# A recurrent mixing block on one core: first sequence in halves, its difference on VectorE, loads in one queue, a new order on all engines

## The reference

```
xn = layernorm(x)                          # over the 128 channels
shifted = xn moved down by one position
k, v, r = mix(xn, shifted, coefficient) @ Wk, Wv, Wr      # r goes through a sigmoid
wkv = recurrence over the 512 positions in k and v (running maximum, numerator, denominator)
s = (r * wkv) @ Wo
h = relu(xn @ w1[0] + b1[0])               # 128 -> 512; the routing weights are 1 for expert 0, 0 for the others
g = silu(layernorm(xn + h @ w2[0] + b2[0]) * gamma + beta)
out = x + s * g
```

## Time and profile before

| What | us |
|---|---|
| median of 3 runs (112.02 to 112.39) | 112.1 |
| span of the profiled execution, first to last instruction | 110.7 |
| PE busy / PE weight loads busy | 101.9 / 56.7 |
| DVE busy | 96.0 |
| ACT busy | 94.3 |
| POOL busy | 66.0 |

### The profile page before, as it was taken

One profiled execution on the slowest core, in us unless ns is written; L12 is line 12 of the kernel. 1 busy time (PEld: TensorE's weight loads), 2 busy tenths in 40 slices (PEclk: granted clock), 3 DMA queues, 4 the chain that ended last, 5 costly groups with the idle time before them and its releaser, 6 DMA issues. The chain is left out here.

```text
span 110.7 us, 1604 instructions
## 1 busy us (share of the span) xinstructions
PE 101.9 (92%) x336; PEld 56.7 (51%) x336; DVE 96.0 (87%) x199; ACT 94.3 (85%) x155; POOL 66.0 (60%) x104
## 2 busy tenths in 40 slices
PE   4997799997999999999999999999999999999660
PEld 4993335553465445553675553674554566435230
DVE  1647989979999999799988989999999897899980
ACT  1425087899999998999899999999999999999940
POOL 3009998986746469459999998743819403360000
PEclk9999999999999999999999999999999999999998
DMA  3999200000000000000002110000000002203134
GB/s 98 284 314 288 61 3 0 0 6 0 0 3 3 0 0 0 0 0 0 0 0 95 46 57 0 0 0 0 3 0 0 3 0 95 81 14 95 46 101 143
DMA packets 9450, 5.09 MB, mean 46 GB/s; under 512 B 481, under 2 KB 9185, under 8 KB 9441
## 3 DMA queue, kind: packets, MB, share of 16 engines
q1 hardware_dynamic: 8880, 4.59, 14.7%
q10 hardware_dynamic: 560, 0.40, 1.3%
HBM read 2.89 MB, written 2.10 MB: 45 GB/s over the span
## 5 line engine op out<-in xcount | busy, mean ns | idle before, releaser
L638 PE MATMUL bank<-hid,w_c 128*128 128x512 f32 x64 | 31.1, 592 | 0.0
L589 PE MATMUL bank<-mixed,w_in 128*128 128x512 f32 x48 | 24.1, 599 | 0.8 <-POOL mixed L379 0.7
L475 ACT ACTIVATE hid<-bank,vec 128x512 f32<-128x512 f32 x32 | 21.4, 683 | 1.1 <-PE bank L611 0.7
L716 DVE SCALAR_TENSOR_TENSOR mixed<-step_x,vec,bank 128x511 f32<-128x511 f32 x24 | 17.5, 738 | 1.6 <-POOL step_x L370 1.6
L638 PEld LDWEIGHTS bank<-hid,w_c 128*128 128x128 f32 x64 | 11.9, 190 | 10.8 <-issue 9.3
L609 PE MATMUL bank<-xT_hi,w_hi 128*128 128x512 f32 x28 | 15.5, 552 | 1.1 <-POOL xT_lo L361 1.1
L589 PEld LDWEIGHTS bank<-mixed,w_in 128*128 128x128 f32 x48 | 8.4, 189 | 10.1 <-issue 8.6
L370 POOL TENSOR_TENSOR step_x<-xT 128x512 f32<-128x512 f32 x8 | 8.3, 1037 | 8.5 <-ACT xT L467 8.4
L403 POOL TENSOR_TENSOR dv<-v_sb 128x512 f32<-128x512 f32 x8 | 9.8, 1227 | 5.8 <-ACT v_sb L526 5.8
L340 POOL TENSOR_SCALAR xn<-x_sb,neg_mean,rstd 128x128 f32<-128x128 f32 x28 | 12.2, 449 | 0.0
L755 DVE TENSOR_TENSOR_SCAN dev<-keep,dv 128x512 f32<-128x512 f32 x8 | 9.8, 1220 | 1.7 <-issue 0.8
(11 more groups left out here) (70 smaller groups left out, 201.3 us busy)
## 6 DMA issues: line engine op xcount, KB each, us to landing
x_sb<-x SPq DMA_DIRECT2D x7, 256.0 KB, 6.6
block_out<-res SPq DMA_DIRECT2D x7, 256.0 KB, 2.3
w_in<-squares SPq DMA_DIRECT2D x1, 256.0 KB, 3.0
w_in<-w ACTq DMA_DIRECT2D x1, 256.0 KB, 5.4
w_in<-w SPq DMA_DIRECT2D x1, 256.0 KB, 6.3
block_out<-res SPq DMA_DIRECT2D x2, 128.0 KB, 1.9
x_sb<-x SPq DMA_DIRECT2D x1, 128.0 KB, 2.2
x_sb<-x ACTq DMA_DIRECT2D x1, 128.0 KB, 2.6
```

What stands on the lines that cost most here:

```text
L475: act.activation(hid[b % 2][:, f, :], ps(f"up{f}", b)[:, :], ACT.Relu, bias=vec[:, B1_COLUMN + f:B1_COLUMN + f + 1]).then_inc(done[f"hid{f ...
L589: pe.matmul(ps(name, b)[:, :], w_in[:, which, :], mixed[b % 2][:, which, :], start=True, stop=True).then_inc(done[name], 1)
L638: pe.matmul(ps("z", b)[:, :], w2_c[:, f, :], hid[b % 2][:, f, :], start=False, stop=chunks_of(b)[-1] == f"z{f}", skip_group_check=True).th ...
L716: dve.scalar_tensor_tensor(mixed[n][:, which, 1:], step_x[n][:, 1:], vec[:, which:which + 1], ps("z", b)[:, 0:T - 1], ALU.mult, ALU.add).t ...
```

## The change

It keeps the arithmetic of every step and changes the following:

- Sequence 0 goes through statistics, aggregation, `ve`, `rs`, `norm1`, transposes and `xT` in two halves `.a` and `.b`; its four `up` products become eight of 256 columns.
- The difference `d:0` moves from GpSimd to VectorE (`d:1` to `d:7` stay on GpSimd).
- `WARM_UP` goes from 11 to 7 and `KEEP_WARM` from 4 to 2; `b2m`, a product of one column, moves ahead of the transposes.
- w1 moves from ScalarE's queue to SyncE's, where it is second; the squares are third, x of sequence 1 fourth, w2 fifth. ScalarE's queue keeps half of x of sequence 0 and the vectors, and gets the store of the second half of the last sequence.
- `PROGRAM` and `BANKS` are new: the same tokens otherwise, in another order on every engine. The four tiny `cols` instructions stand ahead of `norm1` of sequence 0 now.
- Semaphores count per engine and step, so that a step may stand on either engine; functions for `rel`, `hid`, `xT_lo`, `dv` and `xT_hi` on other engines are added, but no token uses them.

```diff
-WARM_UP = 11
-KEEP_WARM = 4
+WARM_UP = 7
+KEEP_WARM = 2
     "pe": """
-        T:0 up3:0 b2m up2:0 k:0 T:1 up0:0 up1:0 v:0 k:1 up1:1 up0:1 up2:1 z0:0 z1:0 T:2 up3:1 z3:0 z2:0
+        b2m T.a:0 T.b:0 up1.a:0 up0.a:0 up1.b:0 up3.a:0 up2.a:0 up2.b:0 up0.b:0 T:1 k:0 up3.b:0 v:0
+        k:1 up0:1 up3:1 r:0 up2:1 z3:0 T:2 up1:1 z3:1 z0:0 z0:1 z1:0 z2:1 up1:2 z2:0 z1:1 k:2 var:0
...
-        z1:6 up3:7 up1:7 z0:6 z3:6 up0:7 back:2 var:6 v:6 s:4 up2:7 back:3 v:7 z0:7 back:4 z1:7 z2:7 r:6
-        r:7 z3:7 s:5 var.a:7 var.b:7 back:5 s:6 s.a:7 back:6 s.b:7 back.a:7 back.b:7
+        var:6 v:6 up0:7 back:3 back:2 z3:7 s:4 v:7 up2:7 r:6 z0:7 z1:7 z2:7 r:7 s:5 var.b:7 var.a:7
+        back:4 s:6 s.b:7 back:5 s.a:7 back:6 back.b:7 back.a:7
     "act": """
-        ln_exp ve:0 rs:0 xT:0 neg_td w1_hi ve:1 rs:1 hid3:0 xT:1 hid0:0 hid2:0 wo hid1:0 v_sb:0 ve:2
-        rs:2 e_keep:0 hid1:1 hid0:1 e_new:0 hid2:1 e_new:1 e_keep:1 xT:2 ln_den:0 hid3:1 ln_den:1
+        ln_exp ve.a:0 ve.b:0 neg_td rs.b:0 rs.a:0 w1_hi xT.a:0 xT.b:0 ve:1 rs:1 wo xT:1 hid1:0
+        hid2:0 hid0:0 hid3:0 v_sb:0 ve:2 rs:2 hid0:1 e_keep:0 hid3:1 e_new:0 hid2:1 e_keep:1 e_new:1
...
     "dve": """
-        bnA:0 bnB:0 aggr1:0 norm1:0 bn:1 aggr1:1 ink:0 w2_sum cols bn:2 bn:3 aggr1:2 mx:0 inv:0 aggr1:3
-        ink:1 gap:0 inr:0 mx:1 bn:4 gap:1 inv:1 den:0 inr:1 den:1 aggr1:4 rel:0 ink:2 rel:1 inv:2 bn:5
+        bn.a:0 bn.b:0 aggr1.a:0 aggr1.b:0 cols norm1.a:0 norm1.b:0 bn:1 aggr1:1 d:0 w2_sum ink:0
+        inv:0 bn:2 bn:3 aggr1:2 mx:0 ink:1 gap:0 aggr1:3 inr:0 mx:1 gap:1 bn:5 inr:1 inv:1 den:0
...
-        inv:7 res:2 den:7 prod:4 rel:6 zn:6 res:3 rel:7 dev:6 adev:6 res:4 wkv:6 dev:7 gated:6 prod:5
-        adev:7 wkv:7 res:5 gated:7 prod:6 zn.a:7 zn.b:7 res:6 prod.a:7 prod.b:7 res.a:7 res.b:7
+        res:3 res:2 rel:7 prod:4 dev:6 adev:6 wkv:6 dev:7 adev:7 gated:6 wkv:7 gated:7 prod:5 res:4
+        prod:6 zn.b:7 res:5 zn.a:7 res:6 prod.b:7 prod.a:7 res.b:7 res.a:7
     "pool": """
-        d:0 w1_lo nm:1 fix:0 norm1:1 w2_c d:1 xT_hi:1 fix:1 xT_lo:1 gmax:0 nm:2 gmin:0 norm1:2 gmin:1
-        gmax:1 dv:0 d:2 xT_hi:2 xT_lo:2 keep:0 fix:2 norm1:3 keep:1 gmax:2 gmin:2 dv:1 d:3 nm:4 xT_hi:3
+        w1_lo nm:1 norm1:1 fix:0 w2_c d:1 xT_hi:1 fix:1 xT_lo:1 gmax:0 nm:2 gmin:0 norm1:2 gmax:1
+        gmin:1 dv:0 xT_hi:2 d:2 xT_lo:2 keep:0 fix:2 norm1:3 keep:1 gmax:2 gmin:2 dv:1 nm:4 xT_hi:3
...
             load_half(sp, 0)
+            sp.dma_start(w1_in[:, :], w1).then_inc(got["w1"], 16)
             sp.dma_start(w_in[:, :, :], squares).then_inc(got["squares"], 16)
...
-            for b in range(B):
...
+            for b in range(LAST):
+                store(sp, b)
+            store(sp, LAST, "a")
...
             load_half(act, 1)
             act.dma_start(vec[:, :], vectors).then_inc(got["vec"], 16)
-            act.dma_start(w1_in[:, :], w1).then_inc(got["w1"], 16)
...
             run("act", steps)
+            store(act, LAST, "b")
...
+            def step_of_x(b):
+                n = b % 2
+                once(dve, b, "edges", EDGES, first_on("dve", "d"))
+                after(dve, "xT", b)
+                for step in ("ink", "inv", "inr", "fix"):
+                    after(dve, step, b - 2)
+                dve.tensor_tensor(step_x[n][:, :], xT[n][:, 1:], xT[n][:, 0:T], ALU.subtract).then_inc(done["dve", "d"], 1)
```

More of the change, by code:

```diff
@@ L42 @@
[L42 to L46, removed]
@@ L68 @@
+        gmax:4 norm1:6 d:5 xT_hi:5 xT_lo:5 dv:3 keep:3 dv:4 keep:4 fix:5 norm1:7 xT_hi:6 xT_lo:6 d:6
+        gmin:5 fix:6 gmax:5 xT_hi:7 d:7 xT_lo:7 fix:7 dv:5 keep:5 gmax:6 gmin:6 gmin:7 gmax:7 dv:6
+        keep:6 dv:7 keep:7
     """,
@@ L73 @@
 BANKS = """
[L74 to L81, removed]
+b2m z:0 r:1 k:3 up0:5 r:4 up3:5 up3:6 k:6 s:5 back:5
+up1:0 r:0 up0:2 up3:2 v:2 k:4 var:4 s:3 up0:6 k:7 var.a:7
+up0:0 k:1 up3:3 z:4 up2:6 r:5 up1:7 up0:7 var.b:7
+up3:0 up0:1 up2:1 up1:1 up1:2 k:2 s:0 up2:4 var:3 v:3 s:2 k:5 var:5 var:6 back:2 up2:7 r:7 s.b:7 back.b:7
+up2:0 up3:1 z:2 z:5 back:3 v:7 s:6 back:6
+z:1 up2:2 up0:3 r:2 up0:4 s:1 back:1 r:3 up1:6 v:5 up3:7 v:6
+k:0 var:0 z:3 back:0 up2:5 z:6 s:4 r:6 back:4 s.a:7 back.a:7
+v:0 var:1 v:1 up2:3 up1:3 var:2 up1:4 up3:4 v:4 up1:5 z:7
 """
@@ L86 @@
             "up2": ["hid2"], "up3": ["hid3"], "var": ["ln_var"], "s": ["prod"], "back": ["res"]}
-HALVED = {"sq", "var", "ln_var", "rstd2", "zn", "silu", "s", "prod", "back", "res"}
+NOT_FOR_FIRST = {"xT_hi", "xT_lo", "nm"}
 def named(token):
@@ L100, in tokens, with signal_table @@
         yield named(token)
+def signal_table():
+    count, table = {}, {}
+    for engine in PROGRAM:
+        for name, half, b in tokens(engine):
+            count[engine, name] = count.get((engine, name), 0) + 1
+            table[name, half, b] = (engine, count[engine, name])
+    return table
 def bank_tables():
@@ L209, in build_block @@
                  "w2_sum", "w2_mean", "w2"]}
[L210 to L216, removed]
+        done = {(engine, name): sem(f"{name}_by_{engine}")
+                for engine, name in dict.fromkeys((signal[token][0], token[0]) for token in signal if token[2] is not None)}
         stored = [sem(f"stored_{n}") for n in range(2)]
@@ L290, in load, with store @@
                           x_rows[b]).then_inc(got[f"x{b}"], 16)
+        def store(eng, b, half=""):
+            after(eng, "res", b, half)
+            eng.dma_start(out_rows[b][:, tiles(half), :], res[b % 2][:, tiles(half), :]).then_inc(stored[b % 2], 16)
         block = ctx.enter_context(nc.Block())
@@ new lines, in aggregate, with normalise @@
+            def aggregate(b, half=""):
+                after(dve, "bn", b, half)
+                for j in range(NT)[tiles(half)]:
+                    ins = dve.bn_aggr(mv1[:, row(b, j), :], stats1[:, row(b, j), :])
+                ins.then_inc(done["dve", "aggr1"], 1)
+            def normalise(b, half=""):
+                after(dve, "rs", b if half else group_of(b), half)
+                after(dve, "T", b - 2)
+                for j in range(NT)[tiles(half)]:
+                    i = row(b, j)
+                    ins = dve.tensor_scalar(xn[b % 2][:, j, :], x_tile(b, j), mv1[:, i, 0:1], rstd1[:, i:i + 1],
+                                            ALU.subtract, ALU.mult)
+                ins.then_inc(done["dve", "norm1"], 1)
@@ L812, in _ @@
             steps.update({"in" + name: mix(name) for name in "kvr"})
+            steps.update({f"hid{f}": hidden(f) for f in range(NF)})
             run("dve", steps)
```

325 lines of the change are left out of this document (179 added, 146 removed).

## The result

| | kernel before | changed kernel |
|---|---|---|
| median, first comparison (4 runs each) | 112.06 us | 112.94 us |
| lowest to highest | 111.56 to 112.39 | 112.78 to 114.11 |
| ratio, 95% interval | | 1.0109 (1.0071 to 1.0148) |
| median, second comparison (33 and 10 runs) | 111.97 | 113.10, 112.25 to 114.51 |
| spans of the second comparison, median and range | 110.1, 109.6 to 110.6 | 111.1, 110.2 to 112.4 |

The change makes the kernel slower by about 1%, and its runs spread over 2.3 us where the kernel before stays within 1.1. The ratios leave out runs more than 1.5% above the fastest of the same kernel, while the medians here are of all runs. The profiled execution of the changed kernel was its fastest of four (112.78) and that of the kernel before one of its longest (110.7), which is why the two spans look alike.

What follows compares the result with a forecast made beforehand. It took full TensorE and ScalarE to bound the middle, with the end set by the dense phase's start. Gains of 0.8 (head), 0.3 (middle) and 0.1 (tail) made 1.2, hence 110.9 us against 112.1, range 109.9 to 112.4.

Steps and rivals of the forecast that it cites:

- norm1.b ends at 6.7, and T.b at 7.4: Sequence 0 in the head: norm1.a begins at 5.6, four tiles take 1.11, then the transposes follow.
- halves, cols and warm-up: Head up to xT:0: halving gains and costs nothing, shorter warm-up makes room; bounds 0.3 us earlier to 0.4 later.
- the clock: TensorE in the head: rise to 2.4 GHz near 10.5, three half products slow, cutting the head's gain from 1.25 to 0.8.
- Rival A: TensorE's clock rises late: 111.9 us at 12.3, 112.7 at 13.6; chance 0.16, half of it slower.
- the tail: From the last silu table load: DVE's 3.9 us backlog just covered; 0.1 gained, close stores up to 0.3 lost.
- the queue of the last store: End of the kernel: the last store's issue no longer queues behind the other half's on SP, 0.1 us gained.
- POOL's paragraph: GpSimd in the head: norm1:1 at 9.5 to 11.25, 1.5 us earlier, since d:0 and w1_lo no longer stand in front.
- hidden, because fix:0 is later: VectorE in the head: ink:0 ends at 10.9, 0.7 later for k:0's input, without cost since fix:0 comes later still.
- the bound: Long middle: PE and ACT full, so it shrinks by at most about 1.3 us; the dense phase's start sets the end.
- the middle: Dense phase: same work per engine, new order spares ACT some idle time; 0.3 us gained, ends -1.3 and +1.3.
- B: Loads: x of sequence 1 lands last in line at 8.5, head's gain only 0.2, giving 111.5 us; chance 0.08.
- C: Dense phase: up products sharing bank 3 wait on ACT's relus; two waits give 112.1 us, a third 112.7; chance 0.12.

Runs made afterwards that it cites:

- b1: Changed kernel with one wait added, so GpSimd starts w1_lo only when VectorE has finished norm1.b:0; 111.29 us, ratio 0.9893.
- a0: The changed kernel run again with nothing altered, as yardstick; 113.10 us, ratio 1.0077.
- a1: Changed kernel with the store of the last sequence's second half issued by SyncE again, ahead of the first half's; 112.71 us, ratio 1.0066.
- a3: Changed kernel with three result buffers in place of two; 112.22 us, ratio 1.0027.
- a2: Kernel before with only the store of the last sequence's second half issued by ScalarE; 112.13 us, ratio 0.9998.
- b4: Changed kernel with w1_lo's wait, the vectors off the path, WARM_UP 11 and KEEP_WARM 4, and three result buffers together; 110.92 us, ratio 0.9887.
- c2: b4 with d:0 moved back to GpSimd, ahead of w1_lo; 111.15 us, ratio 0.9924.
- c3: b4 with the load of w1 back in ScalarE's queue behind the vectors, squares second in SyncE's; 111.10 us, ratio 0.9916.
- c4: b4 with cols moved behind aggr1:1, the statistics of sequence 1, on VectorE; 110.12 us, ratio 0.9817.
- b2: Changed kernel with neg_td behind rs:0 on ScalarE, cols behind norm1.b:0 on VectorE, b2m behind T.b on TensorE; 112.02 us, ratio 0.9915.
- c1: Kernel before with WARM_UP 7 and KEEP_WARM 2, nothing else; 111.89 us, ratio 0.9982.
- b3: Changed kernel with WARM_UP 11 and KEEP_WARM 4 again, nothing else; 112.92 us, ratio 0.9939.

## Why the prediction was wrong

It said 110.9 and 0.71 for faster; 112.94 was measured, outside its range. The step that failed is "norm1.b ends at 6.7, and T.b at 7.4", in the part on halves, cols and warm-up. Its working put four tiles at 1.11 from the earlier trace rows, a row in which GpSimd was idle (it had nothing to do before 8.28), and a paragraph later put w1_lo on GpSimd into the same time, calling it off the path. The trace shows norm1.b at 8.03 and the end of T.b about 8.8; 1.0 us of this is w1_lo, as b1 shows, and the median falls by 1.6 to 1.8 with b1's one wait. In b1's trace up1 comes at 16.72, where the prediction had it (17.53 less 0.8). That it fits so well is partly luck, since norm1 still starts 0.3 late there and the clock rises at 9.6 instead of 10.5. The early w1 and d:0 gone from GpSimd, which had both looked like part of the gain, together made the collision possible: before, w1_hi ran at 8.11 and w1_lo at 9.27, behind d:0.

The second term that was short is the clock, put at 0.45 with the rise at 10.5. The rise was at 10.6, 11.3, 13.6 and 10.3 in four traces of this head (changed, a0, a1, a3). The size was about right for the profiled run, but two things were missed: the late T.b moved the half products to 9.4, so the slow stretch fell on them and the seventh ended at 13.1; and it differs from run to run, 1.64 us between a3 and a1. Rival A gave 111.9 for a rise at 12.3 and 112.7 at 13.6; the measured 112.9 is near its outcome, from a rise near 11 on top of a late norm1 that A did not have.

A named two causes for a late rise, the idle hole ahead of T.a and 8 records fewer. The traces, one execution each:

| TensorE idle just ahead of its transposes | warm-up records | traces | spacing halves for good at |
|---|---|---|---|
| not at all | 22 | before, a2, b4, c2, c3, c4 | 7.4, 4.9, 7.0, 7.0, 4.9, 4.9 |
| 0.52 | 14 | b2 | 6.0 |
| 0.76 | 14 | c1 | about 10 |
| 0.85 | 14 | b1 | 9.6 |
| 0.85, and 0.98 between T.a and T.b | 14 | a0 | 11.3 |
| 1.88 | 14 | changed, a1, a3 | 10.6, 13.6, 10.3 |
| 1.79 | 22 | b3 | about 11.2 |

The prediction expected a hole of 1. Of the traces with a hole only b3 has 22 records, so hole and records are not parted, and that the hole is the cause is my reading of the falls in b3 and a0, not a thing that a run isolates. What the short warm-up costs this kernel is open too: 5 of b3's 12 executions are faster than any of the changed kernel, with the same median.

Third, the tail. The prediction saw DVE's backlog of 3.9 us behind gated:7 and found it just covered, and weighed the nearness of the stores as 0.3 at most. It did not follow res:4's store to the buffer that res:6 needs. Cost 0.4 to 0.8 us by the spans behind up1, 0.9 by the medians of a3 and a0.

Smaller terms: the vectors landed at 5.2, and neg_td and b2m waited for them, so cols ended and norm1 began at 5.9 and not 5.6; d:0 on DVE takes 0.69 (0.65 forecast), but the move is worth about 0.2 on the head of c2, not the 1.5 for which POOL's paragraph took it together with w1_lo; the queue of the last store changes nothing that can be seen (a1, a2), where 0.1 was forecast; k:0 at 13.58 and mx:0 at 14.71 followed T:1, so "hidden, because fix:0 is later" was overtaken by TensorE.

Slips of reading that did not decide: the earlier trace rows shows five sparse slices of ACT, not six; ACT's idle time behind 18.27 is 1.6 us by its own rows (2.35 less 0.7), not 1.3; half of A's 0.16 is 0.08, not 0.07. The 1.4 around the span was 0.5 short, and the profiled span of 110.7 about as much over the median one, which cancel.

What held: the bound. TensorE and ScalarE are full from up1 on, and every profiled execution ends 92 to 93 us behind it, whatever the head did. ACT is idle for 1.3 us from 18.30 to 101.30, against 1.6 before, the 0.3 forecast for the middle. The new order of middle and tail does gain: 0.1 to 0.5 as it stands, 0.9 with a third buffer (93.1 to 92.2), against the 0.4 of the sum. B (x:1 late) did not come: x:1 landed at 6.9 in the profiled execution, and between 6.5 (c4) and 7.7 (a1) in the others. C (a stall in the middle on bank 3) did not come either.

A sum for the changed kernel: the median of 112.94 to 113.10 less 1.95 around the span and 92.8 behind up1 puts up1 at 18.2 to 18.4; the same for 112.0 and 93.1 gives 17.0. That makes the head +1.2 to +1.4, and middle and tail -0.1 to -0.5, together 0.7 to 1.3, where 0.9 to 1.1 was measured. The head's share is worked back from the medians, so the sum is bookkeeping and no test; in the traces up1 lies at 17.5 to 19.2 for the changed head and at 16.7 to 17.5 for the old.

Left open: the halving of sequence 0 was not undone by itself, and the new middle was not run on the old head; its worth is read from traces alone. Nor was b1's wait run together with the third buffer and nothing else.

## What to carry to other kernels

A duration from a row holds for the company in which it was measured. When a reordering puts a VectorE operation on SBUF tiles beside a GpSimd operation for the first time, price the pair and not the two, and try the wait that keeps them apart. When a result is moved later, follow its store to the next writer of the same buffer. And where the dense phase starts is one number that carries the whole head: compare that first, over several executions.

## What was not expected of the hardware

- A VectorE tensor_scalar of 128x128 took 1.28 to 1.37 us beside a GpSimd tensor_tensor of 1.26 us, 0.34 otherwise, and ended 0.08 behind it in five traces of five: a block, not a slow-down.
- TensorE's clock can fall back within the head: in b3 it rose at 4.4, fell at 7.8 behind an idle stretch from 5.7 to 7.5, and rose at about 11.2. The granted clock shows the fall (0.61 and 0.54 by stretch) but reads 1.00 during the first slow stretch, where the spacing is as wide.
- With the same head the rise came between 10.3 and 13.6; that alone moves the dense phase by up to 1.64 us (a3 to a1).
- x of sequence 1 landed between 6.5 (c4) and 7.7 (a1) with the same queue order.
- One store of 256 KB took 2.3 us to land in four traces and 2.8 in two, which moved the end by 0.4 us.
